# Row moments for the second attention taken out of the feed-forward's steady turns

## The reference

```
h = concat(edges(x), txt)
h = h + attention0(layernorm(h))
h = h + feedforward0(layernorm(h))   # silu(x Wg) * (x Wu), then Wd, all quantized to fp4 in blocks of 16
h = h + attention1(layernorm(h))     # 16 heads, softmax over 64 anchors
h = h + experts(layernorm(h))        # one shared expert and one of eight for each row
layernorm(h) = (h - mean) / sqrt(var + eps)
```

## Time and profile before

| | |
|---|---|
| median of 3 runs | 1908.77 us (1907.85 to 1909.83) |
| the profiled execution | 1910.5 us, its span 1908.7 us |
| mean granted TensorE clock | 0.974 |
| busy over the span | PE 93%, PEld 59%, DVE 54%, ACT 36%, POOL 21% |
| feedforward0's steps in the span | about 760 to 990 us |
| `bn_stats` L1307, 24 times | 10.3 us busy |

### The profile page before, as it was taken

How to read it: one execution, slowest core, us unless ns; L and a number is a source line. 1 busy time by engine, 2 the same in 40 slices (tenths; PEclk the granted TensorE clock), 3 DMA queues, 4 the chain that set the end, 5 groups by cost and what they waited for, 6 DMA issues and landing times. The chain is left out here.

```text
span 1908.7 us, 29136 instructions
## 1 busy us (share of the span) xinstructions
PE 1774.1 (93%) x9935; PEld 1121.4 (59%) x9935; DVE 1025.9 (54%) x2071; ACT 679.3 (36%) x1292; POOL 398.9 (21%) x415
## 2 busy tenths in 40 slices
PE   7989999899999994888899999997999999999997
PEld 3324444444444333566665656565666668999997
DVE  6587877777778874788876445542321121222221
ACT  2115656556556673444444223322211110111110
POOL 2101021020210001677662211220032121010010
PEclk9979999999999996999999999998999999999999
DMA  5833643635436023000009000000010012242211
GB/s 186 137 51 64 88 76 39 103 62 65 76 61 91 2 71 126 19 0 0 0 6 375 3 0 0 0 1 1 0 42 33 17 36 97 101 167 99 100 36 32
DMA packets 112675, 117.56 MB, mean 62 GB/s; under 512 B 11535, under 2 KB 104513, under 8 KB 112322
## 3 DMA queue, kind: packets, MB, share of 16 engines
q1 hardware_dynamic: 99330, 87.93, 21.8%
q10 hardware_dynamic: 9600, 18.92, 2.8%
q0 software_dynamic: 3648, 9.46, 1.3%
HBM read 80.87 MB, written 35.29 MB: 61 GB/s over the span
## 5 line engine op out<-in xcount | busy, mean ns | idle before, releaser
L819 DVE TENSOR_REDUCE mx<-ps_a 128x1 f32<-128x384 f32 x768 | 383.6, 551 | 70.0 <-PE ps_a L503 67.8
L706 ACT ACTIVATE prob<-ps_a 128x768 f32<-128x768 f32 (+1 forms) x512 | 306.2, 650 | 119.8 <-PE ps_a L516 119.7
L503 PE MATMUL ps_a<-ks,qs 96*128 96x384 bf16 x768 | 221.6, 340 | 12.0 <-DVE mx L819 4.7
L516 PE MATMUL ps_a<-qs,ks 100*128 100x384 bf16 x768 | 210.3, 334 | 6.5 <-issue 3.8
L2029 PEld LDWEIGHTS ps_e<-xTr,w 128*128 128x128 f32 x1792 | 204.4, 192 | 2.2 <-issue 0.8
L2029 PE MATMUL ps_e<-xTr,w 128*128 128x128 f32 x1792 | 204.7, 275 | 0.6 <-DVE xTr L2202 0.6
L1965 PE MATMUL ps_e<-xT_all,w 128*128 (+1 forms) x512 | 170.4, 492 | 0.9 <-ACT xT_all L2056 0.9
L503 PEld LDWEIGHTS ps_a<-ks,qs 96*128 96x128 bf16 x768 | 61.9, 98 | 181.0 <-DVE mx L819 119.9
L527 PE MATMUL ps_a<-prob,vp 128*32 128x384 f32 x1536 | 164.7, 502 | 0.0
L1514 PE MATMUL ps_m<-w 128*128 128x352 f32 x384 | 125.0, 470 | 21.7 <-ACT w L1677 21.3
L1965 PEld LDWEIGHTS ps_e<-xT_all,w 128*128 128x128 f32 x512 | 97.7, 192 | 66.5 <-issue 1.8
(11 more groups left out here) (242 smaller groups left out, 2519.7 us busy)
## 6 DMA issues: line engine op xcount, KB each, us to landing
ks<-parts_dram SPq DMA_DIRECT2D x192, 96.0 KB, 6.3
w<-in_L_ffn_W_dram ACTq DMA_DIRECT2D x18, 1024.0 KB, 8.2
parts_dram<-parts SPq DMA_DIRECT2D x24, 576.0 KB, 3.9
qs<-parts_dram SPq DMA_DIRECT2D x96, 96.0 KB, 4.2
prob<-in_x_dram SPq DMA_DIRECT2D x24, 256.0 KB, 3.6
w<-in_L_ffn_W_dram SPq DMA_DIRECT2D x6, 1024.0 KB, 13.0
grouped_x<-empty_row SPq DMA_DIRECT2D x1, 4352.0 KB, 24.6
grouped_h<-empty_row SPq DMA_DIRECT2D x1, 4240.5 KB, 33.1
```

The costliest lines, as they stand in the source:

```text
L503: mm = pe.matmul(ps[:, r % 3, 0:T], qs[0:NS, b, u // 2, t * P:(t + 1) * P], ks[0:NS, b, u % 2, u // 2], start=True, stop=True)
L516: mm = pe.matmul(ps[:, 4 + t, 0:T], ks[0:NS + 4, b, kp, hh, t * P:(t + 1) * P], qs[0:NS + 4, b, hh], start=True, stop=True)
L706: act.activation(prob[:, g % 2, j, ts.start:ts.stop], ps[:, 4 + ts.start:4 + ts.stop, 0:T], ACT.Exp).then_inc(exp_done.sem, 1)
L819: dve.tensor_reduce(at, ps[:, r % 3, 0:T], AX.X, ALU.max).then_inc(ring_free.sem, 1)
```

## The change

`EARLY_ROOTS`, the number of tiles whose root is taken first, goes from 18 to 6. `add` no longer holds `bn_stats`; a function `stats(first, end)` does it for several tiles at once. In the last turn, step 0 does tiles 0 to 2 and step 1 tiles 3 to 5, with their `bn_aggr`. The other 18 tiles follow in the passage to attention1, in three groups of six. ScalarE's late `roots` moves ahead of `copy_weights` and `exps`.

```diff
-        EARLY_ROOTS = (B - 2) * TT
+        EARLY_ROOTS = 2 * TT
...
                     dve.wait_ge(dn_done.sem, dn_done.at(i, t + 1))
                     n = i * TT + t
                     dve.tensor_tensor(h[:, n], h[:, n], ps[:, 5, 0:C], ALU.add).then_inc(h_done.sem, 1)
-                    dve.wait_ge(h_done.sem, h_done.at(i, t + 1))
-                    dve.bn_stats(bn[:, n], h[:, n]).then_inc(new_stats.sem, 1)
+
+                def stats(first, end):
+
+                    dve.wait_ge(h_done.sem, end)
+                    for n in range(first, end):
+                        dve.bn_stats(bn[:, n], h[:, n]).then_inc(new_stats.sem, 1)
...
-                        if last and t == 1:
-                            new_moments(0, EARLY_ROOTS)
+                        if last and t < 2:
+                            stats(t * TT, (t + 1) * TT)
+                            new_moments(t * TT, (t + 1) * TT)
...
                 inverses(0, 0, EARLY_ROOTS)
                 inputs1(0, 0)
+                stats(EARLY_ROOTS, EARLY_ROOTS + 6)
                 scaled(0)
                 add(B - 1, 1)
+                stats(EARLY_ROOTS + 6, EARLY_ROOTS + 12)
+                new_moments(EARLY_ROOTS, EARLY_ROOTS + 12)
                 scaled(1)
                 add(B - 1, 2)
-                new_moments(EARLY_ROOTS, NT)
+                stats(EARLY_ROOTS + 12, NT)
+                new_moments(EARLY_ROOTS + 12, NT)
                 less_max(0, 0)
...
                 copy_hidden(B - 1, 2)
+                roots(EARLY_ROOTS, NT)
                 copy_weights(0, 4)
                 exps(0, 0)
                 copy_weights(4, 8)
                 exps(0, 1)
                 exps(0, 2)
-                roots(EARLY_ROOTS, NT)
                 for_pairs(act, turn1)
```

## The result

| | before | changed |
|---|---|---|
| median | 1908.31 us (4 runs, 1900.93 to 1909.83) | 1876.30 us (4 runs, 1873.98 to 1878.73) |
| profiled execution | 1910.5 us, span 1908.7 | 1876.84 us, span 1875.1 |
| ratio | | 0.9845 (95%: 0.9824 to 0.9865) |

By the ratio the kernel got faster by 1.55%, some 30 us. The two medians of the table lie 32.0 us apart; 42 later runs of the kernel before, beside the experiments, have medians of 1903.40 to 1905.88 us.

What follows compares the result with a forecast made beforehand. It took waits through VectorE, not a full engine, to bound the kernel. Steps -21.6 and the rest +1.0 made -20.6 from 1910.5, so 1889.9; the median, 1.7 lower, was 1888.2 us, range 1885.5 to 1899.5.

Steps and rivals of the forecast that it cites:

- What bounds it before: Feed-forward steps: waits through VectorE set the pace; L1267 starting 20 ns behind GpSimd's L1450 costs 1.75 us.
- Steps: Steady feed-forward steps: without `bn_stats` and its wait they fall from 9.735 to 8.6 us, gaining 21.6 us over 19.
- VectorE's ring: Feed-forward steps: the chain of waits through VectorE can shorten to 7.95 to 8.31 us a step.
- TensorE becomes the bound: Feed-forward steps after the change: TensorE's 8.53 us a step, above VectorE's 7.95 to 8.31, sets the pace.
- First step of a pass: First step of each loop pass: the 0.36 us idle on VectorE, put down to `bn_stats` waiting, would be covered.
- Last turn: Last turn's step 0: 1.1 us of added moments fit VectorE's 1.33 us idle, cost 0; later steps gain 0.4 to 1.4.
- Passage: Passage to attention1: second `scaled` 1.7 us late, on TensorE's path; net +0.3 to +1.7, taken as +1.0 us.
- `roots`: ScalarE's late roots ahead of the copies: two table loads go, worth 0, at most 0.4 us.
- The full port: Steps: VectorE and GpSimd take strict turns, so at least 9.1 us a step; 1897.7 us, chance 0.12.
- Only the duration: Steps: the mix of long and short stays, each 0.45 us shorter; 1901.2 us, chance 0.10.
- Slower: Steps: GpSimd holds VectorE so L1267 comes too late and all steps are long; 1923.7 us, chance 0.05.
- Nothing: Steps bound elsewhere, in GpSimd or ScalarE, and 1.7 us at attention1's start eats the rest; about 1908 us, chance 0.03.

Runs made afterwards that it cites:

- experiment 5: Changed kernel plus two `bn_stats` of a constant buffer behind each add of the steady steps, without a wait: 1922.47 us, ratio to before 1.0097.
- experiment 4: Kernel before plus one tiny GpSimd operation ahead of the first rounding of each hidden tile: 1904.22 us, ratio 0.9988.
- experiment 3: Changed kernel plus one `bn_stats` of a constant buffer behind each add of the steady steps, without a wait: 1876.69 us, ratio to before 0.9853.
- experiment 7: Changed kernel with four transposes repeated on TensorE in each feed-forward step: 1883.71 us, ratio to before 0.9886.
- experiment 1: Kernel before, run again unchanged: 1907.62 us.
- experiment 2: Changed kernel with `bn_stats` and its wait for the add put back in the steady steps, result unused: 1907.33 us, ratio to before 1.0004.
- experiment 6: Kernel before with four transposes repeated on TensorE in each feed-forward step: 1905.76 us, ratio 1.0000.
- experiment 10: Kernel before with `bn_stats` taking the tile added one step earlier, so without waiting for the add: 1872.52 us, ratio 0.9832.
- experiment 11: Kernel before with `bn_stats` of the tile added one step earlier, placed between the two gate-times-up products: 1875.39 us, ratio 0.9855.
- experiment 8: Changed kernel with the second `scaled` ahead of the second group of `bn_stats` and `bn_aggr`: 1873.29 us, ratio to before 0.9838.
- experiment 9: Changed kernel with the late `roots` back behind the `exps`: 1877.64 us, ratio to before 0.9856.

## Why the prediction was wrong

*What bounds it before: right.* A race of VectorE's small L1267 against GpSimd's first hidden rounding decides between 8.3 and 10.4 us. Where GpSimd comes at 1.82 us after the step's start, L1267 won at 1.37 (changed kernel) and 1.78 (short steps before) and lost at 1.84 and 1.87 (long steps before, experiment 5). With GpSimd put off to 1.96 (experiment 4) it won at 1.85 and lost at 2.06. In experiment 3 it came at 1.55 against 2.31 and won.

*Steps: the mechanism right, one term too small.* This is the step that failed: "Bounds for a step: 8.53 and 8.9. I take 8.6". It measured 8.20 to 8.31, 8.255 on average. I took one row pair of TensorE, 8.53 us apart, for a step without waits, and so for the least. It held a wait, which TensorE's weight load (PEld) shows and its matmuls don't. The first three rows are of the kernel before, the last is of the changed one.

```profile
781.33 2.46 PEld L1530 LDWEIGHTS ps_m<-w 128*128 128x128 f32 x12 [0.30 <-ACT w L1683]
781.33 2.86 PE L1530 MATMUL ps_m<-w 128*128 128x256 f32 x12
964.91 2.75 PE L1530 MATMUL ps_m<-w 128*128 128x256 f32 x12
```

```profile
784.99 2.76 PE L1539 MATMUL ps_m<-w 128*128 128x256 f32 x12
```

The load of the down product waited 0.30 us for L1683, ScalarE's `copy_hidden`. The product came 2.81 us after the second half began (781.33 - 778.52) and took 2.86; in the changed kernel it comes after 2.59 (784.99 - 782.40) and takes 2.76. These two make up the difference: there the same instructions are 8.20 apart. The kernel before had such a row without the wait as well: the product at 964.91 comes 2.59 us after its second half at 962.32. 19 x (8.6 - 8.255) = 6.6 us of the 13 by which the forecast missed. VectorE's ring I had at 7.95 to 8.31. It was 7.97 to 8.08 in the first steps and 8.30 to 8.33 in the later ones, with one step of 8.73 between them. "TensorE becomes the bound" holds for the first half only: in the last nine steps the ring lies 0.11 above TensorE's 8.20 (experiment 7).

*First step of a pass: right.* The idle of 0.36 went with the wait. It is in the profiles in which `bn_stats` waits for the add before it (experiments 1, 2, 4 and 6) and in none of those without that wait (3, 5, 10 and 11). That the reason is a queue that can't run ahead is my reading; no run shows it.

*Last turn: right.* The added work, which I put at 1.1 us, lies in the idle (1.33 before, 0.46 left).

*Passage: right in kind, too high.* I had 0.3 to 1.7 and took 1.0; it cost 0.25. The place (the second `scaled`) was as said. The raw price was smaller: I had 1.7, TensorE waits 1.15 longer, and experiment 8 gives 1.2 back. Against it stood 1.0 us from the last turn (17.62 against 18.63), inside my 0.4 to 1.4. 0.75 us of the miss.

*`roots`: right*, 0.

*The remaining 5.8 us* of 13.1 between the profiles are 4.65 ahead of the feed-forward and 1.1 behind, in code that is the same. I had no term for it and the range, built on the terms alone, no room. By medians the miss is 12. Most of it lies in the number that I started from. The profiled execution of the kernel before, 1910.5, is slower than each of its 47 other runs (highest 1909.83), and the median of 1908.77 lies 2.9 to 5.4 us above the three later medians of the same kernel. Against those the changed kernel's 1876.30 is 27.1 to 29.6 us less, and steps and passage give 27.9, though the changed kernel itself has no runs beside those. This was bad luck of the reference number and no step of the reasoning. It would have put even a right sum out: with 8.255 and 0.25 in place of 8.6 and 1.0 the forecast would have been 1880.9, 4.6 too high. Experiment 2 fits: with the slow steps back, the change's other text is at before's time. What makes the stretch ahead of the feed-forward spread stays open.

*The rivals.* The full port (0.12) fell: 8.20 a step is under its 9.1. The lock for whole instructions, which the Trainium skill gives on its page "SBUF — State Buffer" in the section "SBUF: two separate sides", is seen in every lost race shown here. But rows of both engines overlap in time, since a held instruction's row holds its wait too (857.47 and 857.42 above), so their sum is no floor. Only the duration (0.10) fell with the changed kernel's own rows, which hold no long step. Slower (0.05) didn't come, but its state exists, 0.70 us of VectorE work a step away (experiment 5). Nothing (0.03) fell with the result.

## What to carry to other kernels

Where a ring passes an exclusive resource, look at the distance between the two engines' arrivals in each repeat, not at busy time: 60 ns there (1.78 against 1.84) were worth 2 us a step, and 0.35 us of added work cost either nothing or 41 us. A wait of an instruction for the one right before it on its own engine can cost more than its 0.15 us: here an idle of 0.36 us in the first step of each pass went with it. Taking the operand of one step earlier, as in experiment 10, removes the wait and keeps the work. A floor for an engine should be summed from its parts where each follows the last without idle, not read off one period.

## What was not expected

More VectorE work made the steps shorter: 8.20 with `bn_stats` in them (experiments 3 and 10), 8.31 in the changed kernel's second half. There, GpSimd is early enough to stand idle for 0.46 us and then starts at 857.42, while the 256 wide multiply comes at 857.47 and ends only at 859.38, a second lost race, by 50 ns. With `bn_stats` GpSimd's instructions and VectorE's come later together, and the multiply wins (886.53 against 886.79), still 0.58 us long. It costs 0.1 us a step, since TensorE's 8.20 lies so near.

The changed kernel passes from one order to the other by a single lost race, of the 44 wide L1267 in the hidden part (L1465 is GpSimd's last hidden instruction):

```profile
827.85 1.39 POOL L1465 TENSOR_TENSOR w<-w 128x704 f32<-128x704 f32 x1 [0.16 <-POOL w L1461]
827.95 1.34 DVE L1267 SCALAR_TENSOR_TENSOR w<-w 128x44 f32<-128x44 f32 x1
```

Up to there GpSimd's first hidden rounding comes 2.12 us after the step's start, the multiply wins at 1.86 and VectorE's steps are 7.97 to 8.08 long. This step takes 8.73, and each one behind it 8.30 to 8.33. What sets it off isn't shown; the same single step of 8.72 to 8.74 stands in experiments 8, 9 and 11, and in neither 3 nor 10.

A won race can lose the next: in experiment 4 the short step only moved.
